# Layer 0's up products as three fp32r products, with a reordered passage to attention and minima taken by a one-operand reduction

## The reference

```python
def _L0_ffn_ref(x, shared_up, shared_down, routed_up, routed_down, router_w):   # 2 shared, 16 routed experts, top 4
    up_s = jnp.einsum('th,seh->tse', xt, shared_up)
    shared = jnp.einsum('tse,she->th', jax.nn.gelu(up_s, approximate=False), shared_down)
    probs = jax.nn.softmax(xt @ router_w.T, axis=-1)
    topk_p, topk_i = jax.lax.top_k(probs, TOP_K)
    gate = jnp.zeros_like(probs).at[jnp.arange(xt.shape[0])[:, None], topk_i].add(topk_p)
    up_r = jnp.einsum('th,reh->tre', xt, routed_up)
    act = jax.nn.gelu(up_r, approximate=False) * gate[:, :, None]
    routed = jnp.einsum('tre,rhe->th', act, routed_down)
    return shared + routed

def _L1_attn_ref(x, ...):                                                        # 16 heads of 64 features
    att = jnp.einsum('bhid,bhjd->bhij', q, k) / DIM_HEAD ** 0.5
    att = att + alibi_bias(S, N_HEADS)[None]
    p = jax.nn.softmax(att, axis=-1)
    out = jnp.einsum('bhij,bhjd->bhid', p, v)
```

## Time and profile before

| | us |
|---|---|
| median of 3 runs | 2289.25 (2287.82 to 2291.89) |
| the profiled execution, its own time | 2301.38 |
| its span, first to last instruction | 2299.4 |
| mean granted clock of PE | 0.984 |
| PE busy | 2191.4 (95%) |
| PE weight loads busy | 1379.6 (60%) |
| DVE busy | 1824.5 (79%) |
| POOL busy | 1386.8 (60%) |
| ACT busy | 1241.9 (54%) |

### The profile page before, as it was taken

The page is one execution under the profiler, slowest core; times in us unless marked ns, Lnnn a source line. Parts: engine busy times, 40 slices in busy tenths (PEclk is TensorE's granted clock), DMA queues, the critical chain, the costliest instruction groups (busy, mean ns, idle before and its releaser), DMA issues.

```text
span 2299.4 us, 40536 instructions
## 1 busy us (share of the span) xinstructions
PE 2191.4 (95%) x10546; PEld 1379.6 (60%) x10547; DVE 1824.5 (79%) x4816; ACT 1241.9 (54%) x1680; POOL 1386.8 (60%) x751
## 2 busy tenths in 40 slices
PE   7989989999999999999999999999999999889995
PEld 4656655565656556565555656555565654449884
DVE  6788786788888888888888888888888887666555
ACT  2333333466666666666566666666666654344442
POOL 2212120677877778787787878777787877543332
PEclk9999999999999999999999999999999999999997
DMA  7050220000001000000100000010000000311114
GB/s 240 24 197 1 85 94 15 22 15 16 13 17 29 21 14 13 19 16 16 31 15 18 14 16 13 16 36 16 14 13 20 14 8 16 144 40 49 47 45 135
DMA packets 90230, 91.25 MB, mean 40 GB/s; under 512 B 22212, under 2 KB 74948, under 8 KB 90120
## 3 DMA queue, kind: packets, MB, share of 16 engines
q1 hardware_dynamic: 85800, 81.35, 11.4%
q0 software_dynamic: 4352, 8.99, 1.2%
HBM read 57.37 MB, written 36.33 MB: 41 GB/s over the span
## 4 chain that ended last, share of the span: by engine, by line
PE 66%; issue 16%; DVE 10%; POOL 4%; ACT 1%; DMA 1%; another core or an unknown queue 0%; POOLq 0%; PEldq 0%; SPq 0%; DVEq 0%; ACTq 0%; PEld 0%
PE P L2030 13%; PE P L2000 9%; PE P L2015 7%; PE P L2016 7%; PE P L2451 3%; PE P L2138 3%; PE P L2124 2%; PE P L2037 2%; PE P L2048 2%; PE P L1951 2%; POOL opair L649 2%; PE P L2421 2%; PE P L2423 1%; PE P L2422 1%; PE P L2441 1%
## 5 line engine op out<-in xcount | busy, mean ns | idle before, releaser
L1640 ACT ACTIVATE big<-P 128x1024 f32<-128x1024 f32 x512 | 512.8, 1021 | 107.6 <-PE P L2016 85.0
L2030 PE MATMUL P<-big,V 128*64 128x512 f32 x2048 | 468.8, 599 | 1.1 <-ACT big L1646 1.1
L649 POOL TENSOR_TENSOR spair<-spair,big 128x1024 f32<-128x1024 f32 x192 | 457.7, 2384 | 16.0 <-DVE hp L809 1.3
L649 POOL TENSOR_TENSOR opair<-opair,big 128x1024 f32<-128x1024 f32 x192 | 457.5, 2383 | 15.0
L1030 DVE CUSTOM_DVE_ANT_0 big<-P,near 128x512 f32<-128x512 f32 x512 | 349.2, 682 | 111.8 <-PE P L2000 108.5
L2000 PE MATMUL P<-kq 96*128 96x512 f32 x1008 | 415.8, 433 | 14.3 <-DVE kq L1014 11.2
L2015 PE MATMUL P<-kq 97*128 97x512 f32 x1024 | 411.9, 402 | 5.7 <-issue 2.8
L1033 DVE TENSOR_REDUCE mhalf<-P 128x1 f32<-128x512 f32 x512 | 349.2, 682 | 78.5 <-PE P L2000 68.1
L2016 PE MATMUL P<-kq 128*128 128x512 f32 x1024 | 409.3, 400 | 0.0
L2000 PEld LDWEIGHTS P<-kq 96*128 96x128 f32 x1008 | 182.0, 190 | 214.3 <-issue 114.1
L2030 PEld LDWEIGHTS P<-big,V 128*64 128x64 f32 x2048 | 135.2, 136 | 265.0 <-issue 262.6
(11 more groups left out here) (316 smaller groups left out, 3665.8 us busy)
## 6 DMA issues: line engine op xcount, KB each, us to landing
slots<-later SPq DMA_DIRECT2D x4, 4224.0 KB, 16.3
kq<-auxrows SPq DMA_DIRECT2D x64, 128.0 KB, 2.3
big<-in_wex SPq DMA_DIRECT2D x8, 768.0 KB
xt<-slots SPq DMA_DIRECT2D x76, 66.0 KB, 1.8
near<-in_aux SPq DMA_DIRECT2D x64, 64.0 KB, 1.8
big<-yrows SPq DMA_DIRECT2D x8, 512.0 KB, 7.2
wqk_hi<-wparts SPq DMA_DIRECT2D x62, 64.0 KB, 1.8
wqk_lo<-wparts SPq DMA_DIRECT2D x62, 64.0 KB, 1.9
```

What stands on the lines that cost most here:

```text
L649: pool.tensor_tensor(psum8[s][:, :], psum8[s][:, :], pfull[:, j % RING, :], ALU.add).then_inc(S["p_added"], 1)
L1640: act.activation(pfull[:, j, :], banks(2 * (j % 2)), ACT.Exp, scale=DH1 ** -0.5).then_inc(S["exp_done"], 1)
L2030: mm = pe.matmul(P[64 * i:64 * i + 64, 4, :], V1[:, j, s, :], half(pfull[:, j, :], i), start=(j == 0), stop=(j == T - 1))
```

## The change

Layer 0's weights of chunks 1 to 8 are copied inside DRAM (wupd), loaded in two pieces (wup_lo), and split once in batch 0: ACT rounds them to fp32r (wup_hi), DVE subtracts (wup_lo). Per batch ACT rounds hT by halves into hb_hi, and DVE subtracts into hb_lo (`up_low`, in `router`). Each up product of chunks 1 to 8 becomes hi x hi + hi x lo + lo x hi. Chunk 0 stays fp32. hb_hi shares its place with h_hi, so POOL's split of h now waits for batch 3's last up product. hb_lo is Qb[1], so batch 1 waits for the store of wparts. Four semaphores are merged into others.

```diff
+    wupd = nc.dram_tensor("wupd", [128, 2, CH0 // 2, 128], F32).ap()
...
-        wup = sb("wup", [128, CH0, 128])
+        wup = sb("wup", [128, 128])
+        wup_lo = [sb(f"wup_lo{i}", [128, CH0 // 2, 128], F32R)[:, :, :] for i in range(2)]
...
-        wqk_hi = [sb(f"wqk_hi{s}", [128, 2 * DH1], F32R) for s in range(2)]
-        wqk_lo = [sb(f"wqk_lo{s}", [128, 2 * DH1], F32R) for s in range(2)]
+        wqk = sb("wqk", [128, 4, 2 * DH1], F32R)
+        wqk_hi, wqk_lo = [wqk[:, s, :] for s in range(2)], [wqk[:, 2 + s, :] for s in range(2)]
+        wup_rest = sb("wup_rest", [128, CH0 // 2, 128], F32R)
...
+        hb_hi, hb_lo = h_hi, Qb[1]
+        wup_hi = [wqk[:, :, :], wup_rest[:, :, :]]
...
+            sp.dma_start(wupd.rearrange("p i c d -> p (i c) d"), a["wup"][:, 1:CH0, :]).then_inc(G["wupd_in"], 16)
...
-            sp.dma_start(wup[:, :, :], a["wup"]).then_inc(G["weights_in"], 16)
+            sp.dma_start(wup[:, :], a["wup"][:, 0, :]).then_inc(G["weights_in"], 16)
+            sp.wait_ge(G["wupd_in"], 16)
+            for i in range(2):
+                sp.dma_start(wup_lo[i].bitcast(F32), wupd[:, i, :, :]).then_inc(G["weights_in"], 16)
...
-            pool.wait_ge(S["x1_done"], EACH["x1_done"] * B)
+            pool.wait_ge(S["up_mm"], EACH["up_mm"] * B)
             pool.wait_ge(S["hT_in"], 16)
             parts_of(hTc, 0)
...
+            def up_low(b, i):
+                if b == 1:
+                    dve.wait_ge(G["wparts_out"], 32)
+                dve.wait_ge(G["hb_hi"], NHALF * b + i + 1)
+                dve.tensor_tensor(half(hb_lo, i), half(hT, i), half(hb_hi, i).bitcast(F32), ALU.subtract).then_inc(G["hb_lo"], 1)
...
+                up_low(b, 0)
                 dve.wait_ge(S[f"{tag}_mm"], b + 1)
                 dve.tensor_reduce(rmax[:, 0, :], logits, AX.X, ALU.max).then_inc(S[f"{tag}_steps"], 1)
                 dve.wait_ge(S[f"{tag}_steps"], steps + 1)
                 dve.tensor_tensor(rlog[:, :, 0:n], logits, col(rmax[:, 0, :], n), ALU.subtract).then_inc(S[f"{tag}_sub"], 1)
+                up_low(b, 1)
                 dve.wait_ge(S[f"{tag}_exp"], b + 1)
...
-                    dve.tensor_tensor(mneg[:, b::4], mhalf[rows, 0, :], mhalf[rows, 1, :], ALU.min).then_inc(S["max_both"], 1)
+                    dve.tensor_reduce(mneg[:, b::4], mhalf[rows, :, :].rearrange("p i t -> p t i"), AX.X, ALU.min).then_inc(S["max_both"], 1)
...
                 if b > 0:
                     c_norms(b - 1)
+                else:
+                    dve.wait_ge(G["wup_parts"], 2)
+                    for i in range(2):
+                        dve.tensor_tensor(wup_lo[i], wup_lo[i].bitcast(F32), wup_hi[i].bitcast(F32), ALU.subtract).then_inc(G["wup_parts"], 1)
...
-                if t == 3:
+                if t == 4:
                     q_low(0, 2, 0)
                     k_low(0, 2, 0)
-                if t == 5:
-                    k_low(0, 2, 1)
-                    q_low(0, 2, 1)
             max_both(1)
             max_rows(1)
+            k_low(0, 2, 1)
+            q_low(0, 2, 1)
...
+                    act.wait_ge(G["weights_in"], W_UP)
+                    for i in range(2):
+                        act.activation(wup_hi[i], wup_lo[i].bitcast(F32), ACT.Copy).then_inc(G["wup_parts"], 1)
                 hT_half(f"b0{b}", 2, modT[:, 4, b:b + 1], modT[:, 3, b:b + 1])
+                act.wait_ge(S["hT_act"], COPY_TAGS[f"b0{b}"] + 1)
+                act.activation(half(hb_hi, 0), half(hT, 0), ACT.Copy).then_inc(G["hb_hi"], 1)
+                act.wait_ge(S["hT_dve"], COPY_TAGS[f"b0{b}"] + 1)
+                act.activation(half(hb_hi, 1), half(hT, 1), ACT.Copy).then_inc(G["hb_hi"], 1)
...
-            c_copies(B - 1)
             q_high(0, 2, 0)
             k_high(0, 2, 0)
+            c_copies(B - 1)
...
-                pe.matmul(P[:, 2 + u % 3, :], wup[:, u // NHALF, :], half(hT, u % 2), start=True, stop=True).then_inc(S["up_mm"], 1)
+                out, i = P[:, 2 + u % 3, :], u % NHALF
+                part, c = divmod(u // NHALF - 1, CH0 // 2)
+                if u < NHALF:
+                    pe.matmul(out, wup[:, :], half(hT, i), start=True, stop=True).then_inc(S["up_mm"], 1)
+                else:
+                    if u < 2 * NHALF:
+                        pe.wait_ge(G["wup_parts"], 4)
+                        pe.wait_ge(G["hb_lo"], NHALF * b + i + 1)
+                    pe.matmul(out, wup_hi[part][:, c, :], half(hb_hi, i), start=True, stop=False)
+                    pe.matmul(out, wup_hi[part][:, c, :], half(hb_lo, i), start=False, stop=False)
+                    pe.matmul(out, wup_lo[part][:, c, :], half(hb_hi, i), start=False, stop=True).then_inc(S["up_mm"], 1)
...
             max_half(1, 1, 2, 1)
+            max_half(1, 1, 3, 0)
             weigh(0, 0, 0, 6)
+            max_half(1, 1, 3, 1)
+            project_qk(0, 2, 0)
+            max_half(1, 1, 4, 0)
+            weigh(0, 0, 0, 7)
+            max_half(1, 1, 4, 1)
             turn(f"c1{B - 1}", 0, xcs[B - 1])
-            project_qk(0, 2, 0)
-            weigh(0, 0, 0, 7)
-            for t in range(3, T):
+            for t in range(5, T):
                 for i in range(NHALF):
                     keep_busy(2, 1)
                     max_half(1, 1, t, i)
-                if t == 4:
+                if t == 5:
                     project_qk(0, 2, 1)
```

More of the change, by code:

```diff
@@ L197, in network @@
         G = {n: ctx.enter_context(nc.semaphore(n)) for n in
-             ("weights_in", "modw_in", "consts_in", "aux_kept", "c_silu", "mod_mm", "modT_mm", "mod_abs", "mod_sgn",
-              "mod_one", "mod_spread", "mod_out", "modT_copied", "set_done", "pool_set", "batch_ended", "batch_open", "x_in", "h_kept", "rows_in", "we_in", "passed", "filled", "wraw_in", "wfc_in", "wparts_out", "scattered0", "scattered1",
+             ("weights_in", "modw_in", "consts_in", "aux_kept", "c_silu", "mod_mm", "mod_abs",
+              "mod_one", "mod_out", "wupd_in", "wup_parts", "hb_hi", "hb_lo", "modT_copied", "set_done", "pool_set", "batch_ended", "batch_open", "x_in", "h_kept", "rows_in", "we_in", "passed", "filled", "wraw_in", "wfc_in", "wparts_out", "scattered0", "scattered1",
               *(f"t_in{i}" for i in range(XBUF)))}
@@ L377, in network @@
         NSET, NPOOL, NCONST = 8, 12, 5
-        W_EARLY, W_PROJ, W_UP, W_ALL = 48, 80, 128, 176
+        W_EARLY, W_PROJ, W_UP, W_ALL = 48, 80, 160, 208
         modrow = wsh[0:B, 0:2 * MODS * D]
@@ L917, in _ @@
             first_norm(h, x0, 1, "f_h")
-            dve.wait_ge(G["mod_spread"], 1)
+            dve.wait_ge(G["mod_mm"], 1)
             dve.wait_ge(S["f_h"], T)
@@ L933, in _ @@
             dve.wait_ge(G["mod_abs"], 3)
-            dve.tensor_scalar(tmp, tmp, 0.25, None, ALU.max).then_inc(G["mod_sgn"], 1)
-            dve.wait_ge(G["mod_sgn"], 1)
-            dve.scalar_tensor_tensor(gs, sg, -1.0, tmp, ALU.add, ALU.mult).then_inc(G["mod_sgn"], 1)
-            dve.wait_ge(G["mod_sgn"], 2)
+            dve.tensor_scalar(tmp, tmp, 0.25, None, ALU.max).then_inc(G["mod_abs"], 1)
+            dve.wait_ge(G["mod_abs"], 4)
+            dve.scalar_tensor_tensor(gs, sg, -1.0, tmp, ALU.add, ALU.mult).then_inc(G["mod_abs"], 1)
+            dve.wait_ge(G["mod_abs"], 5)
             dve.tensor_scalar(r3[:, 1::3, :], r3[:, 1::3, :], 1.0, None, ALU.add).then_inc(G["mod_one"], 1)
@@ L1584, in _ @@
             act.activation(cs[:, :, :], cT[:, :, :], ACT.Silu).then_inc(G["c_silu"], 1)
-            act.wait_ge(G["mod_mm"], 1)
+            act.wait_ge(G["mod_mm"], 2)
             act.activation(modrow, P[0:B, 0:3, :].rearrange("p a b -> p (a b)"), ACT.Copy).then_inc(G["mod_abs"], 1)
-            act.wait_ge(G["modT_mm"], 1)
+            act.wait_ge(G["mod_mm"], 3)
             act.activation(modT[:, :, :], P[:, 3, 0:2 * MODS * B].rearrange("p (m b) -> p m b", b=B), ACT.Copy).then_inc(G["modT_copied"], 1)
@@ L1878, in _ @@
             pe.wait_ge(G["c_silu"], 1)
-            pe.matmul(P[:, 4, 0:2 * D], csb, wmod[:, 0:2 * D], start=True, stop=True).then_inc(G["mod_spread"], 1)
+            pe.matmul(P[:, 4, 0:2 * D], csb, wmod[:, 0:2 * D], start=True, stop=True).then_inc(G["mod_mm"], 1)
             pe.wait_ge(G["c_silu"], 2)
@@ L1886, in _ @@
                 mm = pe.matmul(P[:, 3, m * B:(m + 1) * B], wmod[:, m * D:(m + 1) * D], cs[:, m // MODS, :], start=True, stop=True)
-            mm.then_inc(G["modT_mm"], 1)
+            mm.then_inc(G["mod_mm"], 1)
             pe.wait_ge(G["pool_set"], NPOOL)
```

## The result

The changed kernel takes 2262.99 us (median of 4 runs, 2262.21 to 2264.8), the kernel before in the same comparison 2289.15 (4 runs, 2287.82 to 2291.89): the ratio is 0.988, with an interval of 0.9864 to 0.9896. Forecast were 2259.5, and 2253 to 2275.

The account below looks back on a forecast made before the run. PE, busy 95% of the span, was taken as the bound. Terms 11.2 + 3.1 + 7.3 + 5.5 + 2.7 = 29.8 us bring the median 2289.25 to 2259.5 us, range 2253 to 2275.

Parts of the forecast that it names:

- Minima in the loop: Attention loop: one-input minima are not blocked beside POOL, so PE's seven waits for q_low go, 11.2 us.
- the clock behind two waits: Attention loop: the granted clock falls after two of the seven waits; full clock there gains 3.1 us, bounds 0 and 3.4.
- the clock behind head 1's first scores: After the passage: with PE waiting under 1 us, full clock over 14 gaps gains 2.7 us, bounds 0 and 2.7.
- The new operation's own time: DVE's minima: a 16-element reduction takes about 165 ns, same as now, bounds 163 and 218; nothing charged.
- the 0.25 us of slack: Attention heads: DVE's minima can take 0.25 us longer in all before PE waits.
- Up stage: Layer 0: three fp32r products shorten a unit by 0.155 us; 7.3 us over four batches, bounds 3 and 11.
- the charge of 0.25 for the first group: Up stage, batches 0 to 2: DVE starts behind in a batch's first group, costing 0.25 us.
- the router's charge of 0.27: Router, batches 0 to 2: up_low for half 1 stands in the chain, so the router ends 0.27 us later.
- The 215.7 ns: Up stage: skill's full-clock gap for 512 columns; 58 units would gain 3.3 us more than counted; the sum used 0.234 us.
- Passage: Passage to attention: new order and short minima start head 1 near 423.3 instead of 428.76, 5.5 us, bounds 2.0 and 6.5.
- rival one: Minima stay blocked: loop gives nothing, passage 3.5, up stage 7.3; 10.8 us in all, 2278.5; chance 0.10.
- Costs at nothing: ACT's hT copies, the weights' split and DRAM loads, and POOL's moved split of h were charged nothing.

Follow-up runs that it names:

- second profiles: Both kernels unchanged, profiled again: the kernel before measured 2289.04 us (ratio 1.0002), the changed kernel 2260.58 us (ratio 0.9869).
- min_only: The kernel before with only the one-input minima, a reduction in place of the two-input minimum: 2287.88 us, ratio 0.9925.
- pass_only: The kernel before with only the new order in the passage to attention, on DVE, ACT and PE: 2303.86 us, ratio 0.9989.
- up_only: The kernel before with only layer 0's up products from three fp32r products and what belongs to it: 2297.63 us, ratio 0.996.
- thin_pool: The kernel before with POOL's wo scaling (batches 1 to 3) and splits of the next h cut to 8 columns, minima two-input: 2276.76 us, ratio 0.9944.
- min_pass: The kernel before with the one-input minima and the new order of the passage, up products as before: 2287.13 us, ratio 0.9923.
- long_min: The changed kernel with each of the four minima reading its 16 elements eight times over: 2277.64 us.
- router_early: The changed kernel with DVE's low part of hT's second half moved ahead of the router's chain: 2262.6 us, ratio 0.9873.

## Why the forecast held, step by step

The sum forecast 29.8 us. The parts of it that repeat come to 7.5 + 5.1 + 16.9 = 29.5 between the two second profiles. The median moved by 26.2 in the first comparison and by 28.7 in the second. The forecast took the rest of the program, from head 63 on, as unchanged. It was 391.3 us in the profile that belongs to the 2262.99, 387.8 in that of the 2260.58, and 384.6 in the second one of before: 3 to 7 us longer, which is of the size of the 3.5 us by which 2259.5 was low. That it accounts for them in the medians too is argued from single profiles, not shown. The same part explains the first profile of before, on which the sum was made: of its 12 us over the median it had all there.

**Minima in the loop** (forecast 11.2, and 3.1 for the clock behind two waits): right. All seven waits are gone, and the clock is 1.0 in both stretches. Head 1 to head 63 gains 16.9 us; 11.2 + 3.1 make 14.3, and the missing 2.6 are the clock behind head 1's first scores, which the forecast had counted as 2.7 with the passage. (By its own gaps, 0.44 against 0.234, it would have been 14 x 0.205 = 2.9.) The waits are the minima's work: min_only has the whole gain without the new order. The clock is less firmly tied. All seven profiles with one-input minima have the full clock from head 1 to head 63. Of the five with two inputs, before's two and pass_only are at 1.2 GHz for about 11 us of it, up_only for 3.4 and thin_pool for none. The forecast's condition for the 2.7 us, a wait of under 1 us ahead of head 1's scores, is not what decides: thin_pool waited 2.48 there and kept the full clock. So some of these 5.7 us may be luck. **The new operation's own time** (forecast 165 ns, nothing charged): 160 ns, right, and the 0.25 us of slack that the charge rested on was measured as 0.24 by the waits and 0.19 by the loop.

**Up stage** (forecast 1.65 in each of batches 0 to 2, 2.33 in batch 3, 7.3 in all): measured 1.7 each and 2.34, 7.5 in all. The unit is 1.81 us as forecast, and PE stays the bound. Inside it the charge of 0.25 for the first group shows as the one unit of 2.12 us, 0.3 long, and two terms were off: the router's charge of 0.27 is 0.14, and the first product of the three costs 0.31 and not 0.23 in batches 0 to 2, while the down products before it lead to it sooner (0.81 us from their start, of 1.96 - 0.86 - 0.22 = 0.88 before). The sum of the two is the unit's 0.15. The 215.7 ns of the Trainium skill's page "TensorE: Matmul & The Clock Gate", section "Wait — 56ns, not 53.3ns?", don't show up between these fp32r products, which come 0.23 us apart; the sum by rows was nearer. (Of the units that the forecast counts, 3 x 14 + 15, there are 57 and not 58.)

**Passage** (forecast 5.5): 5.1 and 5.4 in the two pairs of profiles. The shares were not known: 2.9 us come with the minima alone, 0.2 with the order alone, and the two together with the old up stage give 4.8. The order is worth 1.8, and only once the minima are short. The up stage alone gives 1.3, which no term had. The forecast had the gain of both together, but its step "with the block still there the passage gives 3.5" (rival one) was wrong: pass_only gave 0.2, because minima that start earlier wait for more of POOL's additions.

**Costs at nothing.** ACT's copies, the weights' split and the moved split on POOL show no wait of PE. The start is 1.1 to 1.3 us longer in both profiles of the changed kernel. It isn't the change's: min_pass and thin_pool, which leave the start as it was, take 73.4 us to the first gelu, and long_min and router_early, which have the changed start, 71.9 and 71.8. What goes with it is the clock: of the twelve profiles these two of the changed kernel, min_pass and thin_pool have a stretch of 3.4 us at 1.2 GHz from 46 or 47 us on, and no other has.

**Between the stages** 2.9 us came in the second pair of profiles and 0.2 in the first, and no term had counted them. Both kernels run the same work there. The clock differs: for 3.4 us each, the second profile of before is at 1.2 GHz once in each of the three gaps (from 154.2, 242.9 and 331.6 us on), the first in two of them (155.3 and 223.6), and the gaps are 57.1, 54.8 and 56.4 us long against 57.3, 53.4 and 55.0. The changed kernel has such stretches at 131.8 and 305.8, and gaps of 55.9, 53.5 and 56.1. So one of them costs from nothing to 1.5 us, by where it falls. Of the second profiles, before's first stretch and the changed kernel's (columns as above):

```profile
154.20:157.60 3.40, 3.40 (x13) 2.11 (x13) 1.55 (x6) 2.06 (x2) 0.54 (x1) 0.51 1.02 402
```
```profile
131.80:135.20 3.40, 3.40 (x6) 1.58 (x7) 3.01 (x4) 1.79 (x2) 0.00 (x0) 0.50 0.00 0
```

The first catches 13 instructions of PE and the second 6. long_min, with the changed kernel's layer 0, had one at 153.9 again and 57.3 us. I take the 2.9 us as chance; what sets where a stretch falls was not found.

## What to carry to other kernels

Where an engine waits for a short operation that is sometimes fourteen times as long, look at the operation's inputs and at what POOL does just then; a form with one input cures the wait without touching POOL. Two edits can hang together: here the new order was worth nothing until the block had gone, so test it on top of the other and not alone. And before a product is taken out of a stage, work out the unit of the engine next in line, by its order and not by its mean load alone: with two products DVE's load still fitted, but one unit in four waited for it, and half of the saving was lost.

## What the runs showed beyond that

**A block is as long as POOL's instruction, and it comes back.** In pass_only four tiny minima took 5.03 us. Single rows, cut out by narrow stretches, show how:

```profile
423.76 0.16 DVE L1039 TENSOR_TENSOR mneg<-mhalf 32x8 fp32r<-32x8 f32 x1
```
```profile
423.95 2.54 DVE L1039 TENSOR_TENSOR mneg<-mhalf 32x8 fp32r<-32x8 f32 x2
```
```profile
423.93 2.35 POOL L649 TENSOR_TENSOR opair<-opair,big 128x1024 f32<-128x1024 f32 x1
```

The first minimum slips through before POOL's addition of 423.93; the second, 0.02 us behind that addition's start, ends only with it, 2.35 us later; the third goes through the gap of 0.14 us between two additions in 0.16 us; the fourth waits for the whole next addition. Four small operations in a row can so meet two long ones. The Trainium skill's page "SBUF — State Buffer", section "Who interferes with whom", calls the ports that DVE shares with GpSimd an exclusive lock, and says of DVE's two-port modes that whoever issues first has them for the whole instruction and the other is fully blocked. If that goes for a minimum with two inputs as well, these rows agree with it.

**The same program differs by 17 us in a part with no change in it.** From head 63 to the end the twelve profiles have 384.6 to 409.5 us. The four experiments on parts of the change, all on one chip, had 404 to 409.5. It goes with the granted clock (0.96 to 0.93 from the last exponentials on) and with waits for DVE in the shared experts' stage; why it is so was not tried. A profile of before and one of after should be compared by stage before their difference is put down to a change.
